# A Mamba mixer and a factored FFN: modulation in columns, half of the conv taps on TensorE, the last FFN in quarters, and a ring of two

## What is computed

```
mod = silu(c) @ wmod                      # six rows of 512 per batch: sa, ca, ga, sb, cb, gb
ga, gb = sign(ga)*max(|ga|, .25), ...     # gates, kept away from zero
h = layernorm(x)*(1 + ca) + sa
h, gate = split(h @ in_proj)              # 1024 channels each
h = silu(conv(h, 4 taps, causal) + b)     # along the rows, each channel for itself
dt, B, C = split(h @ x_proj)              # 128, 16 and 16 columns
dt = softplus(dt @ dt_proj + b)
s[t] = s[t-1]*exp(-dt[t]*exp(A_log)) + dt[t]*h[t]*B[t]     # 1024 channels x 16 states
y = (sum over the states of s*C + h*D) * silu(gate)
x = x + ga * (y @ out_proj)
x = x + gb * ((layernorm(x)*(1 + cb) + sb) @ sum(factors)/sqrt(8) + bias)
```

## Time and profile before

| | |
|---|---|
| median of 3 runs (lowest to highest) | 1929.47 us (1928.4 to 1930.35) |
| the profiled execution: time, span | 1929.0 us, 1927.3 us |
| busy: PE, DVE, ACT, POOL | 1720.6, 1801.3, 1546.2, 1794.0 us |
| moved by DMA | 186.17 MB, 97 GB/s over the span |

### The profile page before, as it was taken

How to read it: one execution, slowest core, us unless ns; L and a number is a source line. 1 busy time by engine, 2 the same in 40 slices (tenths; PEclk the granted TensorE clock), 3 DMA queues, 4 the chain that set the end, 5 groups by cost and what they waited for, 6 DMA issues and landing times. The chain is left out here.

```text
span 1927.3 us, 29502 instructions
## 1 busy us (share of the span) xinstructions
PE 1720.6 (89%) x9176; PEld 1311.1 (68%) x9176; DVE 1801.3 (93%) x2260; ACT 1546.2 (80%) x4529; POOL 1794.0 (93%) x756
## 2 busy tenths in 40 slices
PE   7995998989899998998989899998989989899798
PEld 4664767667576766767677676766768676676664
DVE  3897999999999999999999999999999999999995
ACT  3776789798888979888787988879788897988773
POOL 1899999999999999999999999999999999999993
PEclk9897999999999999999999999999999999999899
DMA  5756514032140412304042340503213041321310
GB/s 179 258 115 157 145 51 163 24 128 82 55 143 20 152 50 100 110 23 164 23 153 66 116 148 23 165 23 137 72 72 127 34 152 35 104 78 44 111 28 33
DMA packets 72077, 186.17 MB, mean 97 GB/s; under 512 B 6896, under 2 KB 8560, under 8 KB 63984
## 3 DMA queue, kind: packets, MB, share of 16 engines
q1 hardware_dynamic: 68224, 176.94, 27.1%
q0 software_dynamic: 3696, 7.34, 2.4%
HBM read 172.20 MB, written 12.06 MB: 96 GB/s over the span
## 5 line engine op out<-in xcount | busy, mean ns | idle before, releaser
L604 POOL TENSOR_TENSOR ub<-u,b_all 128x2048 f32<-128x2048 f32 x255 | 1166.8, 4576 | 40.7 <-DMA b_all<-bc_scratch 40.7
L756 ACT ACTIVATE decay<-dt,decay_rate 128x256 f32<-128x256 f32 x2048 | 883.7, 465 | 20.4 <-DVE state_p L1548 1.1
L1548 DVE TENSOR_TENSOR_SCAN decay<-decay,ub 128x512 f32<-128x512 f32 x617 | 729.1, 1212 | 21.7 <-ACT decay L756 16.1
L620 POOL TENSOR_TENSOR sc_p<-state_p,c_all 128x1024 f32<-128x1024 f32 (+1 forms) x256 | 499.8, 1952 | 53.1 <-PE y_bank L1088 31.6
L1548 DVE TENSOR_TENSOR_SCAN state_p<-decay,ub 128x512 f32<-128x512 f32 x407 | 480.1, 1207 | 34.5 <-ACT decay L756 32.1
L1088 PE MATMUL y_bank<-ident,sc_d 128*128 128x128 f32 x2468 | 364.6, 279 | 103.6 <-DVE sc_d L1563 103.5
L1088 PEld LDWEIGHTS y_bank<-ident,sc_d 128*128 128x128 f32 x2468 | 289.0, 143 | 180.8 <-DVE sc_d L1563 127.4
L1563 DVE TENSOR_TENSOR sc_d<-decay,c_all 128x512 f32<-128x512 f32 x617 | 395.5, 675 | 7.4 <-PE y_bank L1088 1.7
L742 ACT ACTIVATE carry<-decay 128x2 f32<-128x2 f32 x617 | 99.8, 162 | 220.4 <-DVE sc_d L1563 219.0
L1170 PE MATMUL bank_a<-hT,win_h 128*128 128x256 f32 x992 | 236.3, 384 | 15.3 <-DVE hc L1612 7.8
L1088 PEld LDWEIGHTS y_bank<-ident,sc_p 128*128 128x128 f32 x1628 | 195.6, 145 | 65.5 <-issue 33.2
(11 more groups left out here) (137 smaller groups left out, 1813.3 us busy)
## 6 DMA issues: line engine op xcount, KB each, us to landing
win_h<-win_m SPq DMA_DIRECT2D x128, 256.0 KB, 2.6
win_z<-win_m SPq DMA_DIRECT2D x128, 256.0 KB, 2.7
b_all<-bc_scratch SPq DMA_DIRECT2D x31, 1024.0 KB, 4.7
c_all<-bc_scratch SPq DMA_DIRECT2D x31, 1024.0 KB, 5.1
xa<-x SPq DMA_DIRECT2D x16, 512.0 KB, 5.1
xc<-x SPq DMA_DIRECT2D x16, 512.0 KB, 3.8
out<-xc SPq DMA_DIRECT2D x15, 512.0 KB, 3.7
ffn<-factors POOLq DMA_DIRECT2D x7, 1024.0 KB, 10.1
```

Of the source, the lines that this page charges most:

```text
L604: pool.tensor_tensor(ub[:, slot, :, :, :], u[:, (PAIRS * c + q) % U_PAIRS, :, :].unsqueeze(1).to_broadcast([P, QUAD, 2, ROWS]), b_all[:, n ...
L620: pool.tensor_tensor(sc_p[:, slot:slot + k, :, :], state_p[:, slot:slot + k, :, :], c_all[:, n:n + k, :].unsqueeze(2).to_broadcast([P, k, ...
L756: last = act.activation(bk[:, j * ROWS:(j + 1) * ROWS], dt[:, pair % DT_PAIRS, j, :], ACT.Exp, scale=decay_rate[:, e, n:n + 1])
L1548: dve.tensor_tensor_scan(dst, bk[:, :], ub[:, quad % UB_RING, i, :, :].rearrange("p j r -> p (j r)"), 0.0, ALU.mult, ALU.add).then_inc(sca ...
```

## The change

1. Modulation. `column_mods` multiplies with the weights' columns as the stationary side and the two condition columns as the moving side, so that the result lies in columns at once; `row_mods`, `turn_mods` and the DVE copies of rows go. In front of round 0 `column_mods(2)` and `(3)` stand after `expand_dt` of pair 2; `expand_dt` of pair 3 goes to step 1, and `soft_dt` of pair 1 to step 2 of round 0.
2. `warm_up` puts matmuls of the identity into `y_bank`: 12 at the start, 2 after the modulation, 8 before the last FFN.
3. The order of `project_dt`, `project_b_c`, `expand_dt` and `spread_b` of chunk 0 is changed; ACT copies dt before B and C; tanh of chunk 0's odd pairs goes to `skipped`.
4. Pairs 0 and 1 of later chunks (`T3 = 2`) have tap 0 on PE, with the diagonals `first_diag` that POOL makes at the start; DVE's `taps` has no instruction left for them but still waits for `pre_made`.
5. `U_PAIRS` is 2; `make_u` waits for the products that read the slot before. Pair 3's `make_u` goes from quad 3 to 5, pair 2's from 2 to 3, the next chunk's first from 12 to 11.
6. `shifts` is one operation instead of two.
7. The last FFN waits for each quarter of its input.
8. Steps of several parts move; `EVERY_POOL` is ordered anew.

The core of the diff:

```diff
 DVE_TAPS = 1
+WARM, WARM_H, WARM_L = 12, 2, 8
+T3 = 2
...
 M_AT = (2, 2)
-IN_AT = ((2, 3, 4, 5, 7, 8, 9, 10), (1, 3, 4, 5, 8, 9, 10, 11))
-TAP_AT = ({5: 0, 7: 1, 10: 2, 12: 3}, {5: 0, 7: 1, 11: 2, 13: 3})
+IN_AT = ((2, 3, 4, 5, 7, 8, 9, 10), (1, 2, 3, 4, 8, 9, 10, 11))
+TAP_AT = ({5: 0, 7: 1, 10: 2, 12: 3}, {6: 0, 7: 1, 11: 2, 13: 3})
...
 P_RING = 4
-U_PAIRS = 3
+U_PAIRS = 2
...
 DT_PAIRS = 5
-EVERY_POOL = (2, 2, 1, 1, 2, 2, 1, 2, 2, 2, 2, 1, 2, 2, 1, 1)
+EVERY_POOL = (1, 2, 1, 2, 2, 2, 1, 2, 2, 2, 2, 1, 2, 2, 1, 1)
...
 A_JOBS, A_FREES, C_JOBS = (6, 6), 4, 7
-NORMS = 2 + LB
+NORMS = 3
...
-def dve_taps(c):
-    return DVE_TAPS if c else TAPS - 1
+def dve_taps(c, q):
+    if c == 0:
+        return TAPS - 1
+    return 0 if q < T3 else DVE_TAPS
-    return 2 * (PAIRS * c + q) * DVE_TAPS + 2 * (TAPS - 1 - DVE_TAPS) * (PAIRS if c else q)
+    return 2 * sum(dve_taps(i // PAIRS, i % PAIRS) for i in range(PAIRS * c + q))
...
+def tanh_lane(c, q):
+    return skipped[:, 0, :, :].rearrange("p j r -> p (j r)") if c == 0 and q % 2 else tanh_s[:, :]
...
         pool.wait_ge(dt_made, pair + 1)
+        if pair >= U_PAIRS:
+            pool.wait_ge(ub_made, N // QUAD * (pair - U_PAIRS + 1) - 1)
...
                                conv[:, :, k:k + 1].to_broadcast([P, KE, P]), ALU.mult).then_inc(diag_made, 1)
+        pool.tensor_tensor(first_diag[:, :, :], ident[:, :].unsqueeze(1).to_broadcast([P, 2 * T3, P]),
+                           conv[:, 0:2 * T3, 0:1].to_broadcast([P, 2 * T3, P]), ALU.mult).then_inc(diag_made, 1)
...
                 add_column(c, slice(2, 4), 5)
+            if g == 5:
+                make_u(c, 3)
             multiply_c(quad)
-            if g in (0, 2, 3):
-                make_u(c, max(g, 1))
+            if g in (0, 3):
+                make_u(c, {0: 1, 3: 2}[g])
...
                 scale_ffn(g // 2 - 1)
-            if la is not None and g == 12:
+            if la is not None and g == 11:
...
                 carry_seam(c + 1, 0)
-            if c % PER and g == 4:
+            if c % PER and g == 5:
...
             act.wait_ge(c_free[1], C_JOBS * (c - 2) + 2)
-        if q:
-            act.wait_ge(a_free[(q - 1) % 2], A_FREES * c + 2 + (q - 1) // 2)
-        act.activation(tanh_s[:, :], h_lane(c, q)[:, :], ACT.Tanh).then_inc(tanh_h_made, 1)
+        if q >= (2 if c == 0 else 1):
+            before = q - 2 if c == 0 else q - 1
+            act.wait_ge(a_free[before % 2], A_FREES * c + 2 + before // 2)
+        act.activation(tanh_lane(c, q), h_lane(c, q)[:, :], ACT.Tanh).then_inc(tanh_h_made, 1)
...
     act.activation(warm[:, :], ident[:, 0:1], ACT.Softplus)
+    copy_dt(0)
     copy_bc(0)
-    copy_dt(0)
     soft_dt(0, 0)
-    soft_dt(0, 1)
...
             if c == 0 and s == 2:
+                soft_dt(0, 1)
...
                 make_column(c, 2)
-            if c % PER and s == 12:
+            if c % PER and s == 14:
                 make_column(c, 3)
-            if lc is not None and s in (1, 3, 5):
-                tanh_gate(c - 1, {1: 1, 3: 2, 5: 3}[s])
-            if s in (4, 6, 12):
-                skip(c, {4: 1, 6: 2, 12: 3}[s])
+            if lc is not None and s in (1, 3, 6):
+                tanh_gate(c - 1, {1: 1, 3: 2, 6: 3}[s])
+            if s in (3, 6, 14):
+                skip(c, {3: 1, 6: 2, 14: 3}[s])
...
                     copy_h(c + 1, TAP_AT[c > 0][a])
-                if s == 22:
+                if s == 23:
...
         for k in range(KD):
-            made = act.activation(hT[(FINAL + 1) % H_RING][:, k, t * P:(t + 1) * P], bank_a[t][:, k * P:(k + 1) * P], ACT.Identity,
+            act.activation(hT[(FINAL + 1) % H_RING][:, k, t * P:(t + 1) * P], bank_a[t][:, k * P:(k + 1) * P], ACT.Identity,
                                   bias=mods[:, SB, k, BATCH - 1:BATCH],
-                                  scale=mods[:, CB, k, BATCH - 1:BATCH])
-        made.then_inc(h2_made, 1)
+                                  scale=mods[:, CB, k, BATCH - 1:BATCH]).then_inc(h2_made, 1)
...
         if c == 1 and q == 0:
-            pe.wait_ge(diag_made, len(PE_TAPS))
-        pe.wait_ge(tap_done, tap_start(c, q) + 2 * DVE_TAPS)
+            pe.wait_ge(diag_made, len(PE_TAPS) + 1)
+        if q < T3:
+            pe.wait_ge(pre_made, PAIRS * c + q + 1)
+        else:
+            pe.wait_ge(tap_done, tap_start(c, q) + 2 * DVE_TAPS)
         for j in range(2):
+            if q < T3:
+                pe.matmul(h_lane(c, q)[:, j * ROWS:(j + 1) * ROWS], first_diag[:, 2 * q + j, :],
+                          pre[q % 2][:, j, 0:ROWS], start=False, stop=False, skip_group_check=True)
...
+    def warm_up(times):
+        for _ in range(times):
+            pe.matmul(y_bank[:, 0:P], ident[:, :], ident[:, :], start=True, stop=True)
...
-    def row_mods(j):
+    def column_mods(j):
...
             pe.wait_ge(ub_first, 2 * i + 2)
-        for k in range(KD):
-            last = pe.matmul(bank_c[i][0:BATCH, :], cond_h[:, k, :], staged[i][:, k, :],
-                             start=(k == 0), stop=(k == KD - 1))
+        for m in range(KD):
+            for k in range(KD):
+                last = pe.matmul(bank_c[i][:, m * BATCH:(m + 1) * BATCH], staged[i][:, k, m * P:(m + 1) * P], cond_h[:, k, :],
+                                 start=(k == 0), stop=(k == KD - 1))
-    def turn_mods(i):
-        pe.wait_ge(mods_copied, i + 1)
-        for m in range(KD):
-            last = pe.matmul(bank_c[i % 2][:, m * BATCH:(m + 1) * BATCH], mod_row[i][:, m * P:(m + 1) * P],
-                             ident[0:BATCH, 0:BATCH], start=True, stop=True)
-        last.then_inc(mods_turned, 1)
...
+    pe.wait_ge(consts_made, 1)
+    warm_up(WARM)
     pe.wait_ge(prep, 2)
-    row_mods(0)
+    column_mods(0)
...
     turn_x(0, 1)
-    row_mods(1)
-    turn_mods(0)
-    turn_mods(1)
+    column_mods(1)
+    warm_up(WARM_H)
...
     project_b_c(0, 1)
-    for q in range(2, PAIRS):
-        project_b_c(0, q)
-        project_dt(0, q)
+    project_dt(0, 2)
+    project_dt(0, 3)
+    project_b_c(0, 2)
+    expand_dt(0, 0)
+    project_b_c(0, 3)
     spread_b(0)
-    expand_dt(0, 0)
+    spread_b(1)
     expand_dt(0, 1)
-    spread_b(1)
     expand_dt(0, 2)
-    expand_dt(0, 3)
-    row_mods(2)
-    row_mods(3)
+    column_mods(2)
+    column_mods(3)
...
                 project_gate(c - 1, 2, 1)
-            if lc is not None and s == 25:
+            if lc is not None and s == 26:
...
             if c == 0:
-                if s == 2:
-                    turn_mods(2)
-                    turn_mods(3)
+                if s == 1:
+                    expand_dt(0, 3)
...
                     expand_dt(c + 1, 1)
+                if s == 25:
+                    expand_dt(c + 1, 2)
                 if s == 26:
-                    expand_dt(c + 1, 2)
-                if s == 27:
...
             if lc is not None:
-                for q, at in enumerate((9, 10, 11, 12)):
+                for q, at in enumerate((9, 11, 11, 12)):
...
                         project_out(c - 1, 0, q)
-                for q, at in enumerate((13, 15, 15, 15)):
+                for q, at in enumerate((13, 14, 15, 15)):
...
     project_out_last(1, 3)
+    warm_up(WARM_L)
...
     for t in range(LB):
-        pe.wait_ge(h2_made, t + 1)
         for k in range(KD):
+            pe.wait_ge(h2_made, KD * t + k + 1)
...
         dve.wait_ge(normed, NORMS * c + 2)
-        for t in range(LB):
-            dve.tensor_scalar(nrm[:, 1, t:t + 1], mv[:, t, 0:1], nrm[:, 0, t:t + 1], -1.0,
-                              ALU.mult, ALU.mult).then_inc(normed, 1)
+        dve.scalar_tensor_tensor(out=nrm[:, 1, :], in0=mv[:, :, 0], scalar=-1.0, in1=nrm[:, 0, :],
+                                 op0=ALU.mult, op1=ALU.mult).then_inc(normed, 1)
...
         dve.wait_ge(pre_made, PAIRS * c + q + 1)
-        for k in range(dve_taps(c)):
+        for k in range(dve_taps(c, q)):
...
         wait_u(dve, PAIRS * (c - 1) + q + 1)
-        dve.scalar_tensor_tensor(out=hc[:, 2 * q:2 * q + 2, :].rearrange("p k r -> p (k r)"), in0=tanh_s[:, :],
+        dve.scalar_tensor_tensor(out=hc[:, 2 * q:2 * q + 2, :].rearrange("p k r -> p (k r)"), in0=tanh_lane(c, q),
...
     def copy_mods(i, kind):
-        dve.wait_ge(mods_turned, i + 1)
+        dve.wait_ge(stage_used[i % 2], i // 2 + 1)
-    def copy_mod_rows(i):
-        dve.wait_ge(stage_used[i % 2], i // 2 + 1)
-        dve.tensor_copy(mod_row[i], bank_c[i % 2][0:BATCH, :]).then_inc(mods_copied, 1)
...
     shifts(0, mv_a, nrm_a, norm_a)
-    copy_mod_rows(0)
-    copy_mod_rows(1)
...
                 if s == 1:
-                    copy_mod_rows(2)
-                    copy_mod_rows(3)
-                if s == 3:
...
             if lc is not None:
-                if s in (1, 3, 5):
-                    silu_gate(c - 1, {1: 1, 3: 2, 5: 3}[s])
+                if s in (1, 3, 6):
+                    silu_gate(c - 1, {1: 1, 3: 2, 6: 3}[s])
...
                         gate_sums(c - 1, q)
```

(7 more changed lines are left out.)

## The result

The changed kernel takes 1970.66 us in the median (1962.61 to 1978.95, four runs) against 1929.91 (1928.40 to 1931.70, four): a ratio of 1.0214, interval 1.0188 to 1.0240. The forecast was 1912, in a range from 1896 to 1932. The profiled execution took 1978.95 us (span 1977.2), the longest of the four.

What follows compares the result with a forecast made beforehand. The prediction took DVE as the bound, with POOL and PE close behind. From 1929.0 us it took 15.6 for thirteen rounds, added 0.5 for the start and took 1.7 for the end: 1912 us, range 1896 to 1932.

Steps and rivals of the forecast that it cites:

- Shifts: DVE, twice a round: one operation replacing two saves 0.1 us each time, 0.2 a round (bounds 0 and 0.4).
- Taps and the round: Rounds 2 to 14: taps free 1.73 us of DVE; round shrinks 1.2 us (bounds 1.9 and -0.9), 15.6 in all.
- Moved steps: Steps moved within the rounds issue the same instructions, costing only by where they wait; ACT's `copy_h` within the 0.25.
- The start: Before and in round 0: modulation 1.8, way to the scan -0.6, round 0 -0.7; +0.5 us (bounds -8 and +6).
- +1.8: First modulations on PE: 14.2 us against 12.4, the first block of two-column records fast, the second slow.
- -0.6: Projections to first scan: PE needs five blocks and ACT's copy of B and C instead of six blocks, 0.6 us earlier.
- -0.7: Round 0: second modulations and softplus before the decays, DVE 5 us later or 2 earlier; taps give 1.7 back.
- its idle of 3.47 us before 95.02 covers that: POOL at the start: its first product comes 1.9 us later, absorbed by its later idle of 3.47 us.
- The end: PE's last product: eight warming matmuls before it may save between 0.5 and 2.2 us, taken as 1.7.
- The rivals: Full relief, 1896 us, chance 0.20; PE eats it, 1928 us, 0.12; PE the bound, 1939.5 us, 0.16.
- PE becomes the bound: PE's queue from step 6 to step 18: stretch 0.9 us longer a round, 1939.5 us in all; chance 0.16.
- PE eats the relief: PE's stretch in the rounds: 1.0 us of idle stays, copy of y equally late, 0 a round, 1928 us; chance 0.12.

Runs made afterwards that it cites:

- bias25: The changed kernel with two shift operations, the start of the kernel before, and feed-forward bias and first product back at step 25: 1910.06 us, ratio 0.9908.
- start_bias25: bias25 with the changed start (modulation in columns, new order of first projections, tanhs and copies): 1920.44 us, ratio 0.9957.
- second_rows_bias25: start_bias25 with the second pair of modulations by rows again, the first still in columns: 1916.48 us, ratio 0.9938.
- order_bias25: bias25 with the new order of the start alone, both pairs of modulations by rows as before: 1912.81 us, ratio 0.9917.
- before_taps: The kernel before with only the taps of pairs 0 and 1 on PE, the ring of two and u's places: 1922.49 us, ratio 0.9971.

## Why the prediction was wrong

**Shifts: the step that failed.** "Two small operations become one ... I take 0.1 saved each time, 0.2 a round (bounds 0 and 0.4)". It costs 3 to 4 us a round: 49.5 us on the kernel before, 43.7 in the changed one, which is more than the 38.7 us by which the time lies above the forecast's range. The reason given, that two operations overlap in the pipe, priced DVE alone. I put no bound on the other side, though no row of before showed such an operation beside a working POOL; the taps, which have the same form, read PSUM. The row that should have warned is POOL's 110.6 busy of 114.1 us: what must wait for POOL nearly always does.

What the runs show is how the operation waits. The Trainium skill states this ("SBUF — State Buffer", section "Who interferes with whom"): VectorE and GpSimd share one pair of SBUF ports as an exclusive lock held for a whole instruction, and a VectorE instruction with two inputs in SBUF contends with a GpSimd instruction that reads SBUF. The traces agree: 3.45 us until POOL's product ends at 752.27, 0.67 for `xc`, which has one input in PSUM, and 0.2 for the form with a scalar per partition. The page bore on this change, and I overlooked it.

**Taps and the round: right in sum, not in its parts.** Without the shift and with step 25 as before the round is 112.78 us, forecast 112.9. The window and waits of bias25:

```profile
396.48:509.26 112.78, 105.15 (x579) 81.08 (x577) 109.52 (x136) 96.54 (x287) 110.63 (x47) 1.00 0.26 90
```

```profile
DVE state_p L1571 <- ACT decay L768: 1.5, 2, 1.2
...
DVE decay L1571 <- ACT decay L768: 0.4, 2, 0.2
...
POOL sc_p L628 <- PE y_bank L1099: 1.4, 2, 0.8
```

The agreement is partly luck. Of DVE's relief of 1.9 us, 0.2 was to come from the shift, which is not in this kernel, and the taps free 1.39 us of DVE's busy time (110.91 to 109.52) and not 1.73. The round is shorter by nearly the same, 1.35. The forecast had come to 1.2 another way, as a mean of rounds with and without a fall of PE's clock, less 0.25. POOL is the busiest engine now (110.63), idle 2.15 us of the round, 1.4 of them for PE; no run shows which of the three would bound a further step. The moved steps, which I had at nothing but a share of 0.25, give 0.62 of the 1.35, together with the order of `EVERY_POOL`: without them DVE waits longer for the decays.

**Moved steps, "so they cost only by where they wait": half wrong.** One of them, the bias from 25 to 26, which that list did not name, joins PE's idle at the seam to 2.9 us, the clock falls, and beside the other changes some rounds grow by 3.3 us: 1920.14 to 1910.06 with the old start, 1926.92 to 1920.44 with the new. I had seen a fall after 1.98 us of idle at 643.92, and did not ask which moved step would make such a piece of idle.

**The start: +0.5 taken, some 10 measured, outside the bounds of -8 and +6.** Up to the first scan the sum holds: +1.8 and -0.6 make 1.2, and the first scan of start_bias25 is 1.0 later than that of bias25; in it the first block took 4.83 us and the second 6.83, fast and slow as forecast. In other runs both were slow (6.96 and 6.83 in second_rows_bias25, with the first scan 4.2 later than in order_bias25). Round 0 was mis-sized. The second pair was taken into "-0.7" by halving "5 us later, or 2 us earlier"; it is 2.9 later by the trace, 4.0 by the medians. The order was counted as a gain of 0.6 up to the first scan; the softplus of pair 1 and `expand_dt` of pair 3 come back before the decays of round 0, and it costs some 2 to 3 us. But "its idle of 3.47 us before 95.02 covers that", said of POOL's late first product, is borne out: at that place of order_bias25 POOL's idle has shrunk from 3.10 to 2.32 us and is not gone; it ends at 94.66 instead of 92.45 because the scan of DVE that it waits for is as late.

**The end** was mechanically right: 7.03 us instead of 8.15 for the last product, about 1.5 us in the time, which its interval does not tell from none.

**The rivals.** None of the three was it; the slower one (PE becomes the bound, 1939.5) had the sign but another mechanism, and PE's four more matmuls cost nothing in bias25. PE eats the relief is half seen in before_taps, where 0.73 of DVE's 1.58 us arrive, but what DVE waits for there is ACT's decays. The forecast's sum without the start and the shift would have been 1929.0 - 15.6 - 1.7 = 1911.7; bias25, which is that kernel but for one moved step, has 1910.06.

**Left open:** why the same idle of 2.9 us makes some falls of the clock longer than others, why the same step costs nothing in the kernel before, and what decides whether the first block of columns is slow.

## What to carry to other kernels

Before two instructions become one, compare where their operands lie: here an operation of DVE that reads two tensors from SBUF ended when POOL's running instruction did, whatever its own size, so beside a full POOL give it a scalar operand or one input in PSUM. A step that is moved by one place can join two pieces of PE's idle into one, and then the clock can have its price; look at the longest piece, not at the sum. When a new order makes the first instruction earlier, follow the chain to the next long wait: what was taken out of the way in front may stand there.

## What the runs showed of the hardware

An operation on 128x2 values took 0.15 us at least and 4.50 at most in one kernel, and 30 of 31 ended with the POOL instruction that was running. At the seam, 1.60 us of PE's idle left the granted clock at 1.00 and 2.90 us did not. PE busy in full with two-column matmuls was granted 0.50, the lower of its two levels, where eight 512-column ones at the same place had 1.00. In the first microseconds of a trace the column has to be checked against the matmuls: in bias25 it is at 1.00 from the start, but the first block of eight records, at 8.32, took 5.25 us and the second, of the same shape, 3.59.
